# First attention: result halves copied over 128 partitions, with DMA moves between partitions and new instruction orders

## The reference, cut to what matters

```python
B, S, HID = (1, 256, 256)            # called with 1024 tokens
H, KVH, HD = (32, 8, 64)
q = apply_rope(q); k = apply_rope(k)
k = jnp.repeat(k, groups, axis=1); v = jnp.repeat(v, groups, axis=1)
logits = jnp.einsum('bhqd,bhkd->bhqk', q, k) * scale
logits = jnp.where(causal, logits, jnp.finfo(dtype).min)
attn = jax.nn.softmax(logits, axis=-1)
out = jnp.einsum('bhqk,bhkd->bhqd', attn, v)
return out.transpose(0, 2, 1, 3).reshape(b, s, H * HD) @ Wo.T
```

## Time and profile before

| | us |
|---|---|
| median of 3 runs | 1543.14 |
| lowest and highest | 1541.55, 1544.15 |
| the profiled execution | 1542.92 |
| its span (first to last instruction) | 1541.7 |
| busy in the span: PE, DVE, ACT, POOL | 1455.6, 1131.5, 1024.8, 700.3 |
| granted TensorE clock, mean | 0.978 |

### The profile page before, as it was taken

How to read it: one execution, slowest core, us unless ns; L and a number is a source line. 1 busy time by engine, 2 the same in 40 slices (tenths; PEclk the granted TensorE clock), 3 DMA queues, 4 the chain that set the end, 5 groups by cost and what they waited for, 6 DMA issues and landing times.

```text
span 1541.7 us, 23563 instructions
## 1 busy us (share of the span) xinstructions
PE 1455.6 (94%) x8388; PEld 1216.6 (79%) x8388; DVE 1131.5 (73%) x2487; ACT 1024.8 (66%) x2254; POOL 700.3 (45%) x820
## 2 busy tenths in 40 slices
PE   6999999999999998998999999999999977878898
PEld 5879888888889886786888888888886865655676
DVE  5888889889898975747766766766666659777646
ACT  3898989899898986445655655555554546464654
POOL 5758676666667563134423323323320512722233
PEclk8999999999999999999999999999999998988999
DMA  2000000000000001401000000000005031000000
GB/s 72 18 1 18 1 18 1 18 1 18 1 8 8 8 1 61 200 1 56 22 15 21 15 21 22 15 21 15 2 6 242 19 126 66 0 0 1 1 0 28
DMA packets 14340, 45.12 MB, mean 29 GB/s; under 512 B 3216, under 2 KB 3216, under 8 KB 12048
## 3 DMA queue, kind: packets, MB, share of 16 engines
q1 hardware_dynamic: 14224, 43.61, 7.8%
HBM read 42.55 MB, written 1.05 MB: 28 GB/s over the span
## 4 chain that ended last, share of the span: by engine, by line
PE 67%; DVE 18%; ACT 10%; issue 2%; POOL 1%; DMA 0%; SPq 0%; DVEq 0%; ACTq 0%; POOLq 0%
PE ps L149 27%; PE ps L348 14%; PE ps L1177 8%; PE ps L337 8%; DVE a_pT_lo L404 4%; DVE a_prob L357 3%; ACT a_pT_hi L396 2%; PE ps L1951 2%; PE ps L1957 2%; ACT a_prob L364 2%; DVE a_q L687 2%; ACT a_o_two L656 1%; PE ps L1967 1%; DVE f_r L1567 1%; PE ps L1970 1%
## 5 line engine op out<-in xcount | busy, mean ns | idle before, releaser
L379 POOL TENSOR_SCALAR a_prob<-a_prob,a_rowinv 128x128 f32<-128x128 f32 (+7 forms) x256 | 188.3, 748 | 109.0 <-DVE a_rowinv L373 108.4
L404 DVE TENSOR_TENSOR a_pT_lo<-ps,a_pT_hi 128x512 fp32r<-128x512 f32 (+3 forms) x384 | 195.8, 549 | 25.5 <-ACT a_pT_hi L396 22.5
L364 ACT ACTIVATE a_prob<-a_prob,a_negmax 128x128 f32<-128x128 f32 (+7 forms) x256 | 198.5, 782 | 9.2 <-DVE a_negmax L357 8.4
L379 POOL TENSOR_SCALAR b_prob<-b_prob,b_rowinv 128x128 f32<-128x128 f32 (+7 forms) x128 | 94.3, 749 | 234.6 <-DVE b_rowinv L373 234.6
L357 DVE CUSTOM_DVE_ANT_0 a_prob<-ps,a_mask 128x128 f32<-128x128 f32 (+7 forms) x256 | 188.0, 748 | 13.8 <-PE ps L149 13.5
L396 ACT ACTIVATE a_pT_hi<-ps 128x512 fp32r<-128x512 f32 (+3 forms) x384 | 169.1, 494 | 27.7 <-PE ps L348 15.1
L337 PE MATMUL ps<-ident,a_prob 128*128 128x128 f32 x1152 | 160.4, 275 | 6.8 <-DVE a_pT_lo L404 4.8
L364 ACT ACTIVATE b_prob<-b_prob,b_negmax 128x128 f32<-128x128 f32 (+7 forms) x128 | 99.7, 779 | 82.4 <-DVE b_negmax L357 82.1
L337 PEld LDWEIGHTS ps<-ident,a_prob 128*128 128x128 f32 x1152 | 130.8, 140 | 22.4 <-issue 8.2
L149 PE MATMUL ps<-a_k_hi,a_q 128*128 128x512 f32 (+3 forms) x384 | 140.5, 372 | 2.0 <-DVE a_negmax L357 1.2
L348 PE MATMUL ps<-a_pT_hi,a_v 128*128 128x512 f32 (+3 forms) x384 | 132.0, 351 | 2.4 <-ACT a_o_two L656 1.1
(11 more groups left out here) (452 smaller groups left out, 4138.4 us busy)
## 6 DMA issues: line engine op xcount, KB each, us to landing
f_wq<-in_f_wq SPq DMA_DIRECT2D x2, 2048.0 KB, 8.0
f_wo<-in_f_wo SPq DMA_DIRECT2D x2, 2048.0 KB, 16.8
b_w_raw<-in_b_qk SPq DMA_DIRECT2D x16, 256.0 KB, 2.7
a_w_raw<-in_a_w SPq DMA_DIRECT2D x8, 384.0 KB, 3.2
a_vo<-in_a_o SPq DMA_DIRECT2D x8, 256.0 KB, 2.7
f_wk<-in_f_wk SPq DMA_DIRECT2D x2, 1024.0 KB, 9.9
f_wv<-in_f_wv SPq DMA_DIRECT2D x2, 1024.0 KB, 11.9
f_wg<-in_f_wg SPq DMA_DIRECT2D x2, 1024.0 KB, 19.3
```

Source lines behind the costliest of these rows:

```text
L364: act.activation(prob, prob, ACT.Exp, bias=a.negmax[:, n:n + 1], scale=-1.0, accum_out=a.rowsum[:, n:n + 1]).then_inc(*g.exped.mark(a.tag, u))
L379: pool.tensor_scalar(prob, prob, a.rowinv[:, n:n + 1], 1.0, ALU.mult, ALU.mult).then_inc(*g.normed.mark(a.tag, u))
L404: dve.tensor_tensor(lo, src, fr(hi), ALU.subtract).then_inc(*g.lo.mark(a.tag, u, j0 // 4))
```

## The change

Each result is copied out of PSUM by one instruction over all 128 partitions. An even head's copy goes to `a.o_even[:, qb]`, an odd head's to a new tile `a.o_odd`, of which there is one for both halves of the queries. What stands in the wrong partitions or in the wrong tile is then moved by DMA from SBUF to SBUF, 64 partitions by 512 words (128 KB) each: one move for an even head, two for an odd one, 96 in all. They are issued by SP, which now has 64 `v` steps in its string. POOL's sum waits for the three moves in place of the copies. ACT's copy for an odd head waits, besides, until both moves of the odd result before it have landed, since there is one `a.o_odd`. All orders of the stage were made anew.

```diff
+        self.o_moved = [self.signals("sp", f"o_even_low{b} o_odd_high{b} o_odd_low{b}") for b in range(NH2)]
...
-A_SP = "w" + "wo" * 6 + "oo"
+A_SP = "wwvwovvvvvvvvvwovvvvvvvvwovvvvvvvvwovvvvvvvvwovvvvvvvvovvvvvvvvovvvvvvovvvvvvvv"
...
-        a.o_two = g.sb("a_o_two", [P, NH2, 2, HALF])
+        a.o_even, a.o_off = (g.sb("a_o_" + n, [P, NH2, HALF]) for n in ("even", "off"))
+        a.o_odd = g.sb("a_o_odd", [P, HALF])
...
+            to = a.o_odd[:] if h % 2 else a.o_even[:, qb]
             if h % 2 == 0 and (gr or h):
                 act.wait_ge(*g.o_lo.at(*((gr, h - 1, qb) if h else (gr - 1, A_GRP - 1, qb))))
+            elif h % 2 and (gr or h > 1 or qb):
+                _, gr0, h0, qb0 = a.pairs[a.pairs.index(what) - 1]
+                act.wait_ge(*g.o_moved[qb0][1].at(gr0, h0))
+                act.wait_ge(*g.o_moved[qb0][2].at(gr0, h0))
             act.wait_ge(*g.made.at(a.tag, what))
-            for e2 in range(2):
-                t = act.activation(a.o_two[ROWS[h % 2], qb, e2], g.ps[ROWS[e2], a.side[what], :], ACT.Copy)
-            t.then_inc(*g.copied.mark(a.tag, what))
+            act.activation(to, g.ps[:, a.side[what], :], ACT.Copy).then_inc(*g.copied.mark(a.tag, what))
...
-            both = a.o_two[:, qb]
-            pool.wait_ge(*g.copied.at(a.tag, what))
-            pool.tensor_tensor(both[:, 0], both[:, 0], both[:, 1], ALU.add).then_inc(*g.o_sum.mark(gr, h, qb))
+            for sig in g.o_moved[qb]:
+                pool.wait_ge(*sig.at(gr, h))
+            pool.tensor_tensor(a.o_even[:, qb], a.o_even[:, qb], a.o_off[:, qb], ALU.add).then_inc(*g.o_sum.mark(gr, h, qb))
...
+def attn_a_move_sp(g, a, sp, gr, h, qb):
+    low, high = ROWS
+    sp.wait_ge(*g.copied.at(a.tag, ("val", gr, h, qb)))
+    if h % 2 == 0:
+        if gr or h:
+            sp.wait_ge(*g.o_sum.at(*((gr, h - 1, qb) if h else (gr - 1, A_GRP - 1, qb))))
+        sp.dma_start(a.o_off[low, qb], a.o_even[high, qb]).then_inc(*g.o_moved[qb][0].mark(gr, h + 1, by=16))
+    else:
+        sp.dma_start(a.o_off[high, qb], a.o_odd[low]).then_inc(*g.o_moved[qb][1].mark(gr, h, by=16))
+        sp.wait_ge(*g.o_moved[qb][0].at(gr, h))
+        sp.dma_start(a.o_even[high, qb], a.o_odd[high]).then_inc(*g.o_moved[qb][2].mark(gr, h, by=16))
```

More of the change, by code:

```diff
@@ L470 @@
[L470 to L475 removed]
+    "kkkkkkkkrrrrrrksskksskskststkrststkststststkvsttvstsrrstsstrtstsrstrvsttsvtsssttsttsstsvststvtssttssttssttvstvsstskt"
@@ new lines @@
+    "tsskktstkktsstvkttvsksttosostksrtssttvsrtvtsssrttosrsttossrttvsrtvtsssttssttsstvtstvtsksstsktskttsksktstvkttvsksttos"
+    "osktstrsstvtsrtvtssrsttossrttossrttvsrtvstssttssttsststvtsvtsskttsskktstkskttvtskvtskottssotskstrstsvtsrtvtsssrttosr"
+    "sttossrttvsrtvstssttssttssttvstvsstskttsskkttsskktstvkttvkssttosostkstrststvsrtrsstvsottssrttossrttvsrtvstssttssttss"
+    "tvtstvsstskttksskttsksktstsvkttvskttoosstksrsttssvrttvtsssrttossrttosrstvtstrvsststtssttsstvtstvtssksttsskkttsksktst"
+    "vkttvsksttoosstksrtstsstvrtvtsssrttossrttossrttvsrtvsstststststststvtsvtssttsosttssotsvtsotstsvottssttstsvtstvstsstt"
@@ new lines @@
+    "ststsstvstvtttttttvvoooo")
+A_DVE = (
+    "kkkkkkrrkkrrrrmkmkmikmkmkmlilmkmilmlkmillmrlimlkmimlimlmlmrlmilrmmllrrimlimrmmlimillmmllmlmlimmilmimlillmmllmimllmli"
+    "mmilimlmlmklmlimikkllmkklmlmikimllkmlolmoimlmkilmrlmimlrmillmrllmiommrlloimrlmmrilimllmmllmmlilmlimmilimllmmkmilmlki"
+    "kllmmkkillmkimllkmlolmomikmlilmrlmimlrmillmmrllommirlmloirlmmrliimllmmllmmlimllmiimlmillmmklmlimkikmllkmlklimkimllko"
+    "llmmoimlkmlimrlmimlrmillmmlrlomimrlliomrlmmrilimllmmllmmlilimlmimlmillmmkmlilmkkllimkkmllmikillkmllommomilmkilmrlmim"
+    "lrmmriimllollmmrllomrilmmrliimllmmllmmlilimlmimlmillmmklimlmkikllmmkkllmkimillkmlolimomlmkimlrlmmilrmillmmlrlommirll"
+    "omilmrmlriimllmmllmmlilmlimimlmillmmkmillmkikllmmkkillmkillmkmllooimmlmkimlrlmimlrmillmmlrloimmrlloimrlmmrliimllmmlm"
+    "lmlimllimimlmillmmllmiomilmlmomillmoimmillollmlmlmlimmilmillmmllmmillmlmmiiilllllllloooo")
@@ new lines @@
+A_ACT = (
+    "kkkkkkkkrrrrrrkekekekekehhekrhehkehheehhekevheehhverhrehrehheerherveheeewhhvehheehhweheeveheehhvhheehheehevheehvwhek"
+    "hheewekkhehkkhevhekehhvkehheehekehrhevhreehvherhheerhheewrwhverheehhevhheehheehevheehhwvkeheeehkewkhhkkehehvkehhvekh"
+    "heekehhrehevrheehhvrehheerhheewrwhevrehehhevhheehheehevheeehhvwkhheekewkehhekkhehvkehvhkehheehkehrehevrheehhverhheer"
+    "hheerwwhverehehhevhheehheehevheehwhvekhheeekkwhehkkehehvkehhvkhheeehekherhevhreereehhvehhrhheewrwhevrehehhevhheehhee"
+    "hevheehwhvekhhekeewkhehkkheehvkeehhvkhheehekrhehevrheehhverhheerhheewhwrveehrehhevhheehheehevheehwhvekhheeekkwhhekek"
+    "hehvkehhvkehheehekrhehevhreehhverhheerhheewrwhverehehhevhehehehehehveeehhvwhheeewhheeheheveeehhvhhhheheehveehhwvhhee"
+    "ehhweheeveehvhhhhhhhvvww")
@@ L662, in attn_a_act @@
             act.wait_ge(*g.o_sum.at(gr, h, qb))
-            act.activation(a.oT_hi[:, h // 2, qb * HALF:(qb + 1) * HALF], a.o_two[:, qb, 0], ACT.Copy).then_inc(*g.o_hi.mark(gr, h, qb))
+            act.activation(a.oT_hi[:, h // 2, qb * HALF:(qb + 1) * HALF], a.o_even[:, qb], ACT.Copy).then_inc(*g.o_hi.mark(gr, h, qb))
 def attn_a_dve(g, a, dve):
@@ L765, in attn_a_sp @@
     sp.dma_start(g.f_wr[:], g.ins["f_wr"]).then_inc(*g.f_loaded["wr"].mark(by=16))
-    for kind, what in in_order(A_SP, w=range(1, A_KV), o=range(A_KV)):
+    for kind, what in in_order(A_SP, w=range(1, A_KV), o=range(A_KV), v=a.vals):
         if kind == "w":
@@ L770, in attn_a_sp @@
             attn_a_load_o(g, a, sp, what)
+        elif kind == "v":
+            attn_a_move_sp(g, a, sp, *what[1:])
+def attn_a_move_sp(g, a, sp, gr, h, qb):
[9 more added lines that the diff above has]
+        sp.dma_start(a.o_even[high, qb], a.o_odd[high]).then_inc(*g.o_moved[qb][2].mark(gr, h, by=16))
 def attn_a_load_w(g, a, sp, gr):
```

31 lines of the change are left out of this document (5 added, 26 removed).

## The result

The changed kernel is slower: the ratio of its runs to those of the kernel before is 1.0032, with a 95% interval of 1.0019 to 1.0046. The medians are 1545.2 us against 1541.9 us, 19 runs each. The time lies inside the range, but the forecast was 3.5 us faster. The profiled execution of the changed kernel took 1550.5 us, one of its slower ones, against 1542.9 us before.

A forecast was written before the change was run, and what follows sets the result against it. PE was taken to bound the kernel (414.7 of 420 us busy), ACT next; -5.6 (relief) + 0 (cover) + 2.1 (end) = -3.5 us gave 1539.4 us, 1539.6 for the median. The range ran from half a microsecond under 1534 to 1547 us.

The forecast's parts named there:

- the cap of 11.3 us: PE's idle time from 60 to 590 us in the first attention, claimed as all that can be had there.
- rival (a): All 11.3 us of PE's idle time go, as the new orders also mend other waits; about 1534 us, chance 0.20.
- The copy: ACT's 128 result copies of 592 ns become 64 of 601 ns, taking 37.3 us off ACT.
- The relief, -5.6 us: Gain in the first attention from ACT's shorter copies: 65% taken of 8.6 us, allowing for DVE being next late.
- 8.6 us: ACT's saving on the path: half the copies' chain share, capped by PE's idle time; 1.6 + 5.3 + 1.7 us.
- The queues: SP's moves: 0.43 us an issue, 2.2 us to land, bytes free; weight loads issued behind moves cost nothing.
- Cover in the body, 0 us: Other ACT work hides the moves before the rounding and the next odd copy; bounds 0 to 1.4 us a group.
- The end, +2.1 us: Last group's output starts later: one copy less (-0.6 us), uncovered moves added (0.05 + 0.43 + 2.2 us); bounds 1.5 to 2.6.
- (c): Moves take 2.7 us and land too late, costing 1 us in each of eight groups; 1547.9 us, chance 0.17.
- (b): DVE takes ACT's place, only a fifth of the 8.6 us is kept; 1543.3 us, median 1543.5, chance 0.20.
- (d): The copy is not shorter, since 128 partitions could cost twice 64; given no chance.
- The spread given for the forecast: 1536.4 to 1541.9 us, from 42% to 100% of the relief kept and the bounds on the end's delay.

The follow-up runs named there:

- e8: Kernel before with only ACT's last four steps in the new order (values, values, split, split); ratio 1.0030, median 1543.9 us.
- e9: Changed kernel with the load of the output weights one move step later on SP's queue from the second group on; ratio 1.0035, median 1545.6 us.
- e10: Kernel before, old orders, one 128-partition copy for each pair of copies, no moves (misplaced halves not brought over); ratio 0.9964, median 1536.6 us.
- e7: Changed kernel without moves (misplaced halves not brought over), with ACT's last four steps in the old order; ratio 0.9992, median 1538.2 us.
- e3: Changed kernel without its 96 moves, misplaced halves not brought over, new orders kept; ratio 0.9999, median 1541.4 us.
- e19: Changed copies and moves in the kernel before's orders, but each group's second pair's odd head by two copies, no move; ratio 0.9982, median 1537.3 us.
- e13: Changed kernel with ACT's old last four steps, weight load one move step later, every group's last odd head by two copies; ratio 1.0016, median 1545.5 us.

## Why the prediction was wrong

The account by ratios, in the order of one path from before to after: the copy alone -5.6; the new orders without moves, but with the old last steps, +4.3 (0.9992 - 0.9964); the new last steps +1.1 (0.9999 - 0.9992; e8 alone gives +4.6); the moves +5.1. Sum +4.9. The first is known to 3 us, the others to some 4. By the marks at the end of the stage: -5.3, +2.8, +2.6, +4.7; sum +4.8 (with e9, the same work, in the changed kernel's place, the last is +2.3).

With the clock taken out, as an estimate, the steps are sharper. The mean of time times mean clock over a kernel's runs, less that of the kernel before beside it (1508.9 to 1509.4 us), is -6.2 us for e10, -1.9 for e7, +0.5 for e3; each is known to about 1 us. For the changed kernel it is 1511.7 us, 2.3 to 2.8 us over the kernel before; the result's own runs of that one have no clock listed. So the steps are -6.2, +4.3, +2.4 and about +2.0, and about half of the +4.9 us goes with a lower mean clock, 0.9777 against 0.979 to 0.980. The price of the new orders stands clear of the noise here, where in the ratios it barely does.

- **What bounds the kernel, and the cap of 11.3 us.** PE at 414.7 of 420 us was right. The cap was not: 2.3 of the 5 us that e10 gained had stood as busy time of PE. It decided little: it cut the middle stretch's share from 5.7 to 5.3 us and set rival (a).
- **The copy.** 64 copies of 0.60 us, as forecast (602 ns for even heads, 597 ns for odd ones, on the median); ACT's busy time over the whole span fell from 1024.8 to 984.6 us, 40 us where 37 were worked out.
- **The relief, -5.6 us: right by itself, wrong where it was used.** e10 measured -5.6 us. The failed step is the sentence that the new orders would keep a share between 42% and 100% of 8.6 us, of which I took 65%. I took the orders as a help or as neutral. In the new orders without moves 1.2 us were left (e7), 14% of 8.6, and nothing with their last four steps (e3). The orders give the moves room, and that has a price of its own, +4.3 us. This is half of the 8.4 us between -3.5 and +4.9; the other half is the moves and the last steps, +6.2 us where 0 + 2.1 was forecast. When the group ends are spared the moves, the same work takes 5.2 us less in the old orders than in the new (e19 against e13, 0.9982 and 1.0016).
- **The queues.** Issue 0.46 and 0.60 us against 0.43; landing 2.2, 2.2 and 2.4 us against 2.2; bytes at 32 GB/s, DMA engines 13% busy. All as forecast. The estimate from the Trainium skill (SBUF — State Buffer, "Door 1: The DMA port swizzle" and "The DMA setup-cost knee") was 2.6 us; the trace shows 2.2, and the measurement decides. "A load issued behind moves costs nothing" looked at the wrong direction: it is the moves behind a load that land late, though e9 found no price for it.
- **Cover in the body, 0 us.** For ACT it holds (2.8 us of stands at the rounding). For POOL it does not, 27.7 us in 22 waits, with divisions queued behind. Between the kernel without moves (e3) and the two with them (e9 and the changed kernel) the last value product is 1.3 to 3.7 us later: inside my bounds of 0 to 1.4 us for each of eight groups, not at their lower end. This term was put too low. One small slip: the cover of the wait at the odd copy adds up to 3.5 us, not 3.6.
- **The end, +2.1 us.** Measured 2.9 us (11.7 against 8.8). The mechanism was another. I had costed the landing, and had not looked at the order of ACT's last four steps, though it stands in the string. It costs 2.3 to 2.6 us by itself, part of it through the lower clock behind the longer stand; with it in place a landing is half hidden, since the rounding waits for the second copy in any case: from the last value product to the end it takes 10.7 us in e3, without moves, and 11.7 with them.
- **The rivals.** As a change against the kernel before, +4.9 us, the time came out at (c), +5.0, the moves landing too late, but not by its mechanism: a move took 2.2 us, not 2.7, and ACT hardly stood at `w`. The median, 1545.2 us, is nearer to (b)'s 1543.5 than to (c)'s 1547.9, and (b) had a fifth of the relief kept, close to the 14% of e7. Whether DVE took ACT's place is less clear: PE's waits for DVE's maxima, its two rows taken together, grew from 8.2 to 11.6 us, but DVE itself stood longer for PE. (d) was rightly given nothing. The spread given for the forecast, 1536.4 to 1541.9 us, takes the late tail at its upper end but not the early one at its lower; with 1.5 us it would begin at 1535.8. My last sentence on what would make me most wrong, that PE's time hangs on the orders more than on ACT's load, names what happened.

## What to carry to other kernels

A relief on a second engine, worked out from the chain, can be sound and still not arrive when the orders are changed to pay for something else: cost the new order as an item of its own, with the cheap change in the old order as the base. Before moving everything, ask which of the transfers is waited for by an engine with other work queued behind it; here keeping a quarter of the results on the old copies made new orders needless. And read the last few steps of every engine's string at the end of a stage: one exchange of two steps moved the end of the stage by half as much as the whole change did. And when executions of one kernel differ by 10 us, look at the clock listed with each: here time times mean clock told apart what the times alone could not.
